# Cross attention in 64 by 64 tiles, with keys two batches ahead through a scratch in device memory

## The reference, cut to what matters

```python
# second (l1x)
Q, K, V = queries @ W_q.T, keys @ W_k.T, values @ W_v.T      # by heads: b h s 16
scores = jnp.einsum('bhqd,bhkd->bhqk', Q, K) / scale
scores = jnp.where(mask, scores, NEG_INF)
out = softmax(scores) @ V, heads joined, @ W_proj.T + b_proj
# fourth (l3x)
q = _l2norm(x @ Wq + bq) * scale_mul;  k = _l2norm(y @ Wk);  v = y @ Wv
attn = softmax(einsum('bhqd,bhkd->bhqk', q, k) + attn_bias)   # attn_bias 64 x 1601
out = attn @ v, heads joined, @ Wo + bo
```

## Time and profile before

| | us |
|---|---|
| median of 3 runs | 2486.56 |
| lowest, highest | 2485.36, 2490.42 |
| the profiled execution | 2501.07 |
| its span | 2499.3 |
| mean granted clock of TensorE | 0.971 |

### The profile page before, as it was taken

One profiled execution on the slowest core, in us unless ns is written; L12 is line 12 of the kernel. 1 busy time (PEld: TensorE's weight loads), 2 busy tenths in 40 slices (PEclk: granted clock), 3 DMA queues, 4 the chain that ended last, 5 costly groups with the idle time before them and its releaser, 6 DMA issues. The chain is left out here.

```text
span 2499.3 us, 50978 instructions
## 1 busy us (share of the span) xinstructions
PE 2236.3 (89%) x20593; PEld 1417.7 (57%) x20650; DVE 1650.0 (66%) x3182; ACT 1243.2 (50%) x2071; POOL 808.3 (32%) x660
## 2 busy tenths in 40 slices
PE   6885779999978889999999999699879999998898
PEld 4764445666654555656655666356546555566554
DVE  4987456555548756888888854644576666665577
ACT  2326234555554225555555554566436555563565
POOL 5610052233206112321233300045445455433254
PEclk8998899999989989999999999899999999999999
DMA  3200453423313047676776764133322323220231
GB/s 113 71 7 1 144 136 103 107 78 106 79 66 106 13 118 144 121 133 133 151 146 122 125 113 80 34 102 102 116 67 67 86 69 86 69 67 23 71 96 60
DMA packets 358618, 226.84 MB, mean 91 GB/s; under 512 B 289913, under 2 KB 326610, under 8 KB 358386
## 3 DMA queue, kind: packets, MB, share of 16 engines
q1 hardware_dynamic: 355314, 215.20, 35.5%
q0 software_dynamic: 3072, 8.39, 1.2%
HBM read 114.87 MB, written 0.52 MB: 46 GB/s over the span
## 5 line engine op out<-in xcount | busy, mean ns | idle before, releaser
L3950 POOL TENSOR_TENSOR l2x_rows<-l2x_rows,l2x_one 128x256 f16<-128x256 f32 (+1 forms) x91 | 89.2, 1006 | 379.6 <-DVE l2x_rows L1507 354.5
L100 PE MATMUL PS<-hot 128*128 128x512 f16 x460 | 134.3, 427 | 82.1 <-DVE l0a_g L1119 17.5
L4054 PE MATMUL PS<-l2x_rows,l2x_pth 128*128 128x512 f16 x832 | 200.3, 379 | 1.7 <-DVE l2x_mean L4263 1.7
L3711 DVE CUSTOM_DVE_ANT_0 l1x_junk<-PS,l1x_bias 128x1024 bf16<-128x1024 f32 (+1 forms) x128 | 123.2, 991 | 73.6 <-PE PS L3371 72.7
L4256 DVE TENSOR_TENSOR l2x_pl<-l2x_sc,l2x_ph 128x1664 f16<-128x1664 f32 x64 | 125.1, 1954 | 44.6 <-ACT l2x_ph L4133 43.9
L4151 ACT ACTIVATE l2x_meanT<-PS 128x256 f32<-128x256 f32 x64 | 24.5, 383 | 250.5 <-PE PS L4016 250.5
L4241 DVE CUSTOM_DVE_ANT_0 l2x_sc<-PS,l2x_bias 128x1665 f32<-128x1665 f32 x64 | 120.9, 1889 | 36.3 <-issue 35.0
L3711 DVE CUSTOM_DVE_ANT_0 l3x_junk<-PS,l3x_bias 128x1024 bf16<-128x1024 f32 (+1 forms) x128 | 123.6, 991 | 24.3 <-PE PS L3371 21.6
L4008 PE MATMUL PS<-l2x_kh,l2x_qth 128*128 128x512 f16 (+1 forms) x512 | 131.9, 339 | 1.5 <-issue 1.5
L4008 PE MATMUL PS<-l2x_kh,l2x_qtl 128*128 128x512 f16 (+1 forms) x512 | 131.9, 339 | 0.0
L4008 PE MATMUL PS<-l2x_kl,l2x_qth 128*128 128x512 f16 (+1 forms) x512 | 131.9, 339 | 0.0
(11 more groups left out here) (866 smaller groups left out, 6109.0 us busy)
## 6 DMA issues: line engine op xcount, KB each, us to landing
l2f_unit<-in_L_ffn_units_dram SPq DMA_DIRECT2D x36, 384.0 KB, 3.1
l3f_unit<-in_L_ffn_units_dram SPq DMA_DIRECT2D x34, 384.0 KB, 3.0
l1x_kst<-l1x_kh SPq DMA_DIRECT2D x128, 100.1 KB, 2.2
l3x_kst<-l3x_kh SPq DMA_DIRECT2D x128, 100.1 KB, 2.2
l2x_rows<-in_ctx_dram SPq DMA_DIRECT2D x8, 1536.0 KB
l1x_ctx<-in_ctx_t_dram SPq DMA_DIRECT2D x7, 1601.0 KB, 7.3
l3x_ctx<-in_ctx_t_dram SPq DMA_DIRECT2D x7, 1601.0 KB, 7.0
l1x_kst<-l1x_kl SPq DMA_DIRECT2D x64, 100.1 KB, 2.2
```

Of the source, the lines that this page charges most:

```text
L100: self.nc.tensor.matmul(self.PS[:, bank, :], self.hot[:, 0:P], self.hot[:], start=True, stop=True)
L3711: v.tensor_tensor_reduce(junk[:, slot(it), 0:n], slot_banks(it)[:, 0:n], bias[:, 0 if normed else b % 2, at:at + n], 1.0, LOWEST, ALU.add, ...
L3950: last = nc.gpsimd.tensor_tensor(high[:, at], of[:, at], one[0:p, at].unsqueeze(2).unsqueeze(3).to_broadcast([p, i, NC, P]), ALU.mult)
L4054: nc.tensor.matmul(PS[:, ACC, :], pth[:, u % 2, m, :], rows2[:, b % 2, :, :, m, :], start=(m == 0), stop=False)
```

## The change

- Scores in 64x64 tiles. A head has its own 49 rows (16 high, 16 low, a row of constants at 32, 16 high), even heads on partitions 0 to 48 and odd ones from 64. `A` becomes 16 items of two units by a quarter of the keys (401 or 398 columns), each four matmuls on the four corners of the array, read by DVE in two operations. `turned` makes both groups at once, in 32 matmuls of 64 columns, g now being the head of the pair.
- The queries are made in this layout as float16 and turned by matmuls with a float16 identity; no masked copies.
- Keys are made two batches ahead. kh and kl are written to a scratch in device memory (`spill`) and read back into kst when its half is free. K, N, I and U get b + 2 in `steps`; batch 0 has its own tables, `opening_steps` and `second_keys`.
- l1x: mask on TensorE for every m; DVE adds none. l3x: the TensorE bias is in two parts (high, low), so two matmuls per tile.
- ACT and DVE: both exponentials (or adds) of a step, then the items of both half-steps. The context is split by halves.

```diff
-    A = [("A", u, h) for u in range(R) for h in range(NH)]
+    A = [("A", v, j) for v in range(QV) for j in range(NCH)]
@@ steps of l1x (K_[0..3]: K; V_: V; A: maxima)
-        steps = [[("K", 0, 0)], [], [("K", 0, 1), R_], [("K", 1, 0)], [E], [("K", 1, 1)], [("V", 0, 0)], [O_], [A[0]], [A[1]],
-                 [("V", 1, 0), A[2]], [A[3]], [P_, A[4]], [("V", 2, 0), A[5]], [A[6]], [A[7]], [("V", 3, 0), A[8]], [A[9]],
...
+        steps = [[V_[0]], [], [R_], [V_[1]], [E], [V_[2]], [V_[3], A[0]], [O_, A[1]], [A[2], A[3]], [A[4]], [A[5]], [A[6]], [P_, A[7]],
+                 [A[8]], [K_[0]], [A[9], M_[0]], [A[10]], [K_[1]], [A[11]], [A[12]], [K_[2]], [A[13]], [A[14]], [A[15], K_[3]], [],
+                 [M_[1]]]
@@ steps of l3x
+        steps = [[V_[0]], [], [R_, V_[1]], [], [E], [V_[2]], [V_[3]], [O_], [A[0]], [A[1], A[2]], [A[3]], [A[4]], [P_, A[5]], [A[6], A[7]],
+                 [K_[0]], [K_[1], A[8]], [N_[0], M_[0]], [N_[1], I_[0], A[9]], [U_[0], I_[1], A[10]], [U_[1], K_[2], A[11]],
+                 [K_[3], A[12]], [N_[2], A[13]], [N_[3], I_[2], A[14], A[15]], [U_[2], I_[3]], [U_[3]], [M_[1]]]
@@ SP: keys out to the scratch, and back into kst
+                    for x, part in enumerate((kh, kl)):
+                        sp.dma_start(spill[x, c], part[:, c, :]).then_inc(spilled[c], 16)
...
+                    for at, x in ((0, 0), (DH, 1), (ROW + 1, 0)):
+                        for r in range(2):
+                            sp.dma_start(kst[r * S + at:r * S + at + DH, b % 2, c * RC:(c + 1) * RC, :],
+                                         spill[x, c].rearrange("(j r d) n -> r d j n", r=2, d=DH)[r]).then_inc(stacked[c], 16)
@@ PE, item A
-                        for i, at, n in pieces(*halves[j]):
-                            last = nc.tensor.matmul(PS[:, bank + i, 0:n], qst[0:3 * F, b, c, :, :],
-                                                    kst[0:3 * F, b % 2, c, at:at + n], start=True, stop=True)
+                        for i in range(2):
+                            for r in range(2):
+                                rows = slice(r * S, r * S + KROWS)
+                                last = nc.tensor.matmul(PS[i * S:(i + 1) * S, bank + r, 0:n], qst[rows, b, 2 * c + i, :],
+                                                        kst[rows, b % 2, 2 * c + i, at:at + n], start=True, stop=True)
@@ PE, turned
-                            pe.wait_ge(exp_done, e - G2 + 1)
+                            pe.wait_ge(exp_done, e)
                     if m == 0:
-                        pe.wait_ge(row_made, G2 * b + g + 1)
+                        pe.wait_ge(row_made, G2 * (b + 1))
...
-                        nc.tensor.matmul(PS[0:n, S_BANK + g, :], of_bias, one_hot[:], start=True, stop=False)
-                    for i in range(UG):
...
+                        for x in range(2 if normed else 1):
+                            for at, w_ in keys:
+                                for r in range(2):
...
+                    for u in range(R):
+                        for at, w_ in keys:
+                            for r in range(2):
+                                rows = slice(r * S, r * S + KROWS)
+                                last = nc.tensor.matmul(PS[at:at + w_, S_BANK + r, u * S:(u + 1) * S],
+                                                        kst[rows, b % 2, u, m * P + at:m * P + at + w_], qst[rows, b, u, :],
@@ DVE, item A
+                        for r in range(2):
+                            last = v.tensor_tensor_reduce(junk[:, slot(it), r * BANK:r * BANK + n], PS[:, 2 * slot(it) + r, 0:n],
+                                                          bias[:, 0 if normed else b % 2, at:at + n], 1.0, LOWEST, ALU.add, ALU.max,
+                                                          rmax[:, r, c, j:j + 1])
```

More of the change, by code:

```diff
@@ L2996, in context_attention @@
     G2 = 2
-    UG = R // G2
+    ROW = 32
+    KROWS = 3 * DH + 1
+    QCOLS = 64
+    CHUNK = -(-NK // 4)
+    chunks = [(at, min(CHUNK, NK - at)) for at in range(0, NK, CHUNK)]
+    NCH = len(chunks)
+    QV = R // 2
     VW = DH + 1
     Q4 = P // 4
-    HG = H // G2
     VT = 4
@@ L3008, in context_attention @@
     ONE_HOT = 2.0 ** 6 if normed else 1.0
-    ON_VECTOR = list(range(4))
+    ON_VECTOR = list(range(4)) if normed else []
     def vector_count(b, m, g):
@@ L3324, in item @@
                             pe.wait_ge(q_dve, c)
-                        for r in range(c * RC, (c + 1) * RC):
+                        pe.wait_ge(unit_made, 1)
+                        pe.wait_ge(q_blank, 1)
+                        for u in range(c * RC, (c + 1) * RC):
                             for t in range(NT):
-                                last = nc.tensor.transpose(PS[0:3 * F, Q_BANK + r % RC, t * P:(t + 1) * P], q3[:, t, r, :, :],
-                                                           k.ident[:])
+                                last = nc.tensor.matmul(PS[:, Q_BANK + u % RC, t * P:(t + 1) * P], q3[:, t, u, :], ident16[:],
+                                                        start=True, stop=True)
                         last.then_inc(q_turned, 1)
@@ L3411, in turned @@
                     on_tensor = m not in ON_VECTOR
+                    keys = [(at, min(S, n - at)) for at in range(0, n, S)]
                     if on_tensor:
-                        of_bias = fsp[:, m * P:m * P + n] if normed else bias[:, b % 2, m * P:m * P + n]
-                        nc.tensor.matmul(PS[0:n, S_BANK + g, :], of_bias, one_hot[:], start=True, stop=False)
-                    for i in range(UG):
-                        u = g * UG + i
-                        last = nc.tensor.matmul(PS[0:n, S_BANK + g, i * P:(i + 1) * P], kst[:, b % 2, u, m * P:m * P + n],
-                                                qst[:, b, u, :, :], start=not on_tensor,
-                                                stop=not on_tensor or i == UG - 1)
@@ L3420, in turned @@
-                    last.then_inc(turned_made, 1)
+                        for x in range(2 if normed else 1):
+                            for at, w_ in keys:
+                                for r in range(2):
+                                    half = slice(r * S, (r + 1) * S)
+                                    of_bias = fsp[half, x, :] if normed else bias[half, b % 2, :]
+                                    nc.tensor.matmul(PS[at:at + w_, S_BANK + r, :], of_bias[:, m * P + at:m * P + at + w_], one_hot[half, :],
+                                                     start=(x == 0), stop=False, skip_group_check=True)
@@ new lines, in turned @@
+                    for u in range(R):
[4 more added lines that the diff above has]
+                                                        kst[rows, b % 2, u, m * P + at:m * P + at + w_], qst[rows, b, u, :],
+                                                        start=not on_tensor, stop=not on_tensor or u == R - 1, skip_group_check=True)
+                                if u == R - 1 and at == keys[-1][0]:
+                                    last.then_inc(turned_made, 1)
@@ L3429, in values @@
                         pe.wait_ge(v_read, b * NV + m // VT + 1)
-                    for i in range(HG):
-                        h = g * HG + i
-                        at = (h % 4) * Q4
-                        last = nc.tensor.matmul(PS[at:at + VW, PV_BANK + b % 2, (h // 4) * S:(h // 4 + 1) * S],
-                                                v33[0:n, b % 2, m, h, :], pT[0:n, (b * KT + m) % 2, g, i * S:(i + 1) * S],
-                                                start=(m == 0 and h < 4), stop=(m == KT - 1), skip_group_check=True)
+                    for u in range(R):
+                        at = (u % 4) * Q4
+                        block = 2 * g + u // 4
+                        last = nc.tensor.matmul(PS[at:at + VW, PV_BANK + b % 2, block * S:(block + 1) * S],
+                                                v33[0:n, b % 2, m, 2 * u + g, :], pT[0:n, (b * KT + m) % 2, g, u * S:(u + 1) * S],
+                                                start=(m == 0 and block == 0), stop=(m == KT - 1), skip_group_check=True)
                     last.then_inc(summed, 1)
@@ L3753, in _ @@
                                 add_bias(b, m, g)
-                            for it in step_before(b, m * G2 + g):
+                        for g in range(G2):
+                            for it in at_step(b, m * G2 + g):
                                 item(it)
```

253 lines of the change are left out of this document (138 added, 115 removed).

## The result

| | before | after |
|---|---|---|
| median, us (lowest to highest) | 2488.5 (2485.4 to 2492.3) | 2799.1 (2792.9 to 2801.5) |
| ratio, 95% interval | | 1.124 (1.122 to 1.127) |
| span of the profiled execution | 2499.3 | 2799.8 |
| l1x, first to last score matmul | 340.3 | 457.1 |
| l3x, first to last score matmul | 394.3 | 570.1 |

The kernel became 12% slower, 311 us. Slower was forecast, but by 20 us: the time lies far outside the range.

A forecast was written before the change was run, and what follows sets the result against it. TensorE, busy 89% of the span, was taken as the bound. +9 us in l1x, +15 in l3x and -4 in prologues made +20 on 2501.1, so 2521 profiled and a median of 2507 us; range 2440 to 2560.

The forecast's parts named there:

- The scratch: hidden.: Key copies through device memory: asked for at the batch's start, needed 11 us later, so hidden from batch 1 on.
- A items waiting on DMA: Sign named beforehand that would show the forecast wrong: score-maxima items held up by transfers.
- The clock is at its full level, so rates can be carried over.: TensorE in the trace of before: 2.4 GHz throughout, so its measured rates were applied to the changed kernel.
- Rates: TensorE costs taken from trace rows: 32 transposed-score matmuls 0.26 us a step, a score-maxima item 0.17.
- Rival B: Score blocks: column tiles over the same rows don't load together, a round costs 56 ns or more; +60 us, 2547; chance 0.18.
- switches: TensorE's changes of tile shape, 0.1 us each: some 15 more a batch in l1x, 18 in l3x; 1.5 and 1.8 us lost.
- The walk through a steady batch: Step-by-step sum of hand-overs: 46.7 us against 46.3 in l1x, 53.5 against 53.8 in l3x; TensorE's gain becomes waits.
- Chain (1): Each step: joint score block, then both exponentials before the next; at least 1.85 us in l1x, 2.04 in l3x with double bias.
- Batch 0: Each layer's first batch, carrying two batches of keys in l1x, early keys' round trip in l3x: 55.7 and 81 us.
- Prologues: Before each layer's batches: float16 query transposes and fewer masked copies, less added switches; -2 us a layer, -4 in all.

The follow-up runs named there:

- e11: The kernel after with score tiles of 64 rows by 128 columns, the order of work of before, and no key transfers after batch 1; ratio 1.031.
- e8: The kernel after with score tiles of 64 rows by 128 columns and no key transfers after batch 1; ratio 1.052.
- e1: The kernel after without key transfers for batches 2 to 7, the stale stacked keys being used again; ratio 1.073.
- e5: The kernel after with mask and score tiles of 64 rows by 128 columns, 16 matmuls a step instead of 32; ratio 1.087.
- e4: The kernel before with its keys written to a scratch in device memory and read back in transfers of 32 partitions; ratio 1.050.
- e2: The kernel after with stacked keys copied straight from kh and kl in SBUF, 48 transfers a batch, no device memory; ratio 1.110.
- e9: The kernel after with the odd heads' key reads issued by ScalarE on its own queue, from batch 2 on; ratio 1.118.

## Why the prediction was wrong, by its steps

The 309 us in a chain of kernels, of which each after e11 changes one thing (each difference good to some 7 us); the first step holds all the rest of the change, small tiles and joint wait together:

| from | to | us |
|---|---|---|
| before | e11: 64x128 tiles, old order, no key transfers | +77 |
| e11 | e8: keys two batches ahead | +51 |
| e8 | e1: 64x64 tiles | +54 |
| e1 | after: the key transfers | +127 |

- **"The scratch: hidden."** The step that failed first. The size was off: a burst of 23 us a batch for the reads, where I had 6 in for each half, 12 in all. The start was off in l3x: the reads are issued 5 to 8 us into the batch, since the write before them waits for GpSimd's split, a term that the sum put at nothing. So the keys are not hidden there even where nothing stops TensorE (e5: 6.7 to 7.8 us of waiting a batch), and the prediction's sign "A items waiting on DMA" came. And above all the question asked was only when the keys are needed. The transfers fill the engines that also bring TensorE's instructions: 93 us of stops, and +127 in all with what hangs on them.
- **"The clock is at its full level, so rates can be carried over."** Wrong: 331 us of these layers ran at half clock. Before 37 of the 38 falls TensorE had stood idle for 1.0 us or more at a stretch, in a stop or a wait, shortly before; the fall at 808.2, in l1x's last batch, had no wait over 0.5. But such a wait alone does not bring a fall: e1's second batch has one of 2.2 us and six of the batches of before in l1x one of 1.58 (as at 440.92 in the earlier trace rows), at 1.00 throughout. What decides is open. Half clock makes each other cost larger, and how much of each difference it is was not separated.
- **Rates.** Right: 32 score matmuls in 0.26, A 0.17, mask 0.24. Rival B is refuted. But "switches" counted only those between blocks; 16 more stand inside the block of 65 keys, about 24 us, and no term looked at how 1601 divides.
- **The walk through a steady batch** held for steps 0 to 10 in l1x and not for the rest: e1's undisturbed batch of l1x takes 49.3 against 46.7, its batches of l3x 61.5 to 64 against 53.5. e1's step times in l1x against the forecast: steps 0 to 2, 12.0 (11.8); 3 to 6, 10.1 and 11.8 (11.0); 7, 6.8 (6.7); 10, 4.2 (4.3); then 11, 6.3 to 8.5 (5.6), and 12, 4.4 to 4.7 (2.7), the last block's 1.9. In l3x step 7 is 6.8 (6.8), but 8 is 6.3 (4.6) and 10 is 9.6 to 12.1 (8.3), where K3 waits for VectorE's copy.
- **Chain (1).** Right: steps of the last batch are 1.86 (1.85), its sums without the last block's fault 24.4 and 26.3 (24.5 and 26).
- **Batch 0.** Too small: 71.1 and 108.5 against 55.7 and 81. In l3x A0 waits for the first read keys, PE in the timeline:

```profile
2038.30 0.88 PE L3422 MATMUL PS<-l3x_kst,l3x_qst 49*64 49x401 f16 x8 [13.61 <-DMA l3x_kst<-l3x_spill]
```

  It comes 51.0 us into the batch, where 43 was forecast, and 71 us go to its last five steps, with K, N and A items all in them; 45 us of the batch are at half clock. e11's batch 0 has 52.5 and 72.1.
- **Prologues.** l1x's first score matmul came 6.5 us earlier, but in e4, whose prologue is before's, 7.6 earlier too, so this shows no gain; from l1x's last score matmul to l3x's first it is 13 us more, where 2 less were forecast.

No version made here beats the kernel before. e11, which has no key transfers after the first two batches, is slower too, so mending these alone would not have been enough.

## What to carry to other kernels

Before moving traffic to a place where nothing waits for it, look at what else uses the DMA engines there: TensorE's instructions come over them, 256 at a time, and small tiles use them up faster. When a stop is gone, look again at the wait that it hid: here the keys were late too. Look at the remainder of a dimension before cutting it in tiles, since a tile of another width in the middle of a block costs more than the block. And where two tile halves share one wait, put the waiting beside what side by side saves, before crediting TensorE's time.

## What the runs showed of the hardware

- A stop of TensorE without a semaphore that always begins at the same place modulo 256 instructions was a late fetch here; in DMA bursts of 23 us a fetch began up to 14.7 us after its boundary, and the reserve was one group of 256. With the engines busy 0.40 of the time (e2) none caused a stop.
- Four 64x64 tiles, two of which share rows, run all at once: 32 matmuls in 0.26 us, 32 ns a round.
- Between a pair of tiles of 64 columns and a pair of 1 column, in either order, 117 or 143 ns pass; rounds of one shape follow in 32.
- Reads from device memory into 16 partitions ran at 99 to 157 GB/s, into 32 partitions at 154 to 265; two queues that filled 16 each at once shortened a burst by 1 to 2 us of 22.5 (e9).
